# Reordering the vector engine's work around the layer-norm scale, and the first weights, in a routed adapter kernel

## What is computed

```python
h = gelu(x @ W_down[role] + b_down[role])        # 1024 -> 512, exact gelu
u = h @ W_up[role] + b_up[role]                  # 512 -> 1024
y = x + u
mean, var = mean(y), mean((y - mean) ** 2)       # over the 1024 columns
x = (y - mean) * rsqrt(var + 1e-5) * gamma[role] + beta[role]
```

## Time and profile before

| what | value |
|---|---|
| time, median of 3 runs | 2749.48 us (2748.82 to 2749.53) |
| time of the profiled execution | 2748.52 us |
| its span | 2746.7 us |
| mean granted clock of TensorE | 0.992 |
| PE busy | 2686.8 us, 98% |
| DVE busy | 2209.5 us, 80% |
| ACT busy | 1669.8 us, 61% |
| POOL busy | 1388.9 us, 51% |
| down matmuls on PE (L517), each of three kinds | 812 to 813 us |
| HBM traffic | 207 GB/s over the span |

### The profile page before, as it was taken

One profiled execution on the slowest core, in us unless ns is written; L12 is line 12 of the kernel. 1 busy time (PEld: TensorE's weight loads), 2 busy tenths in 40 slices (PEclk: granted clock), 3 DMA queues, 4 the chain that ended last, 5 costly groups with the idle time before them and its releaser, 6 DMA issues.

```text
span 2746.7 us, 54496 instructions
## 1 busy us (share of the span) xinstructions
PE 2686.8 (98%) x11714; PEld 2207.3 (80%) x11714; DVE 2209.5 (80%) x3357; ACT 1669.8 (61%) x2905; POOL 1388.9 (51%) x1050
## 2 busy tenths in 40 slices
PE   8999999999999999999989999999989999999997
PEld 6888888887788888888768888888778888888885
DVE  6777777778777777777898888888888888888886
ACT  4666656666666665665656656665656566665664
POOL 1455555455555555555545454454444455545545
PEclk9999999999999999999999999999999999999998
DMA  6656656566665666656756566666756665666654
GB/s 224 211 193 215 212 199 213 203 230 227 216 215 201 206 209 205 214 199 225 243 185 223 193 215 213 196 212 206 250 184 216 200 223 195 217 204 203 216 190 149
DMA packets 360582, 573.29 MB, mean 209 GB/s; under 512 B 40144, under 2 KB 239952, under 8 KB 359248
## 3 DMA queue, kind: packets, MB, share of 16 engines
q1 hardware_dynamic: 358704, 554.14, 60.3%
q10 hardware_dynamic: 1440, 15.47, 1.5%
HBM read 364.97 MB, written 204.47 MB: 207 GB/s over the span
## 4 chain that ended last, share of the span: by engine, by line
PE 88%; DVE 6%; issue 4%; ACT 1%; DVEq 1%; POOL 0%; DMA 0%; ACTq 0%; POOLq 0%; SPq 0%
PE pD L517 47%; PE bX L529 23%; PE bZ L529 18%; DVE wul L863 1%; DVE xt L961 1%; DVE hl L943 1%; DVE xT L914 1%; DVE wdl L844 0%; DVE xt L953 0%; DVE xl L921 0%; DVE hT L928 0%; DVE xt L984 0%; ACT wdh L601 0%; ACT pC L705 0%; DMA xt<-in_itok 0%
## 5 line engine op out<-in xcount | busy, mean ns | idle before, releaser
L517 PE MATMUL pD<-wdh,xh 128*128 128x512 f32 x2080 | 813.2, 391 | 18.9 <-DVEq L905 18.9
L517 PE MATMUL pD<-wdl,xh 128*128 128x512 f32 x2080 | 812.1, 390 | 0.0
L517 PE MATMUL pD<-wdh,xl 128*128 128x512 f32 x2080 | 812.0, 390 | 0.0
L462 POOL TENSOR_TENSOR xt<-xt,cgb 128x1024 f32<-128x1024 f32 x258 | 629.1, 2439 | 348.7 <-ACT xt L713 348.7
L470 POOL TENSOR_TENSOR cs<-hT 128x256 f32<-128x256 f32 x130 | 154.0, 1185 | 907.4 <-DVE hT L928 907.4
L705 ACT ACTIVATE pC<-xt,nmean 128x512 f32<-128x512 f32 x520 | 358.9, 690 | 260.6 <-DVE nmean L969 251.6
L713 ACT ACTIVATE xt<-xt,rstd 128x1024 f32<-128x1024 f32 x258 | 296.5, 1149 | 319.3 <-POOL rstd L448 315.6
L517 PEld LDWEIGHTS pD<-wdh,xh 128*128 128x128 f32 x2080 | 392.2, 189 | 103.7 <-DVEq L905 16.5
L517 PEld LDWEIGHTS pD<-wdh,xl 128*128 128x128 f32 x2080 | 392.2, 189 | 82.0
L517 PEld LDWEIGHTS pD<-wdl,xh 128*128 128x128 f32 x2080 | 392.3, 189 | 81.5
L529 PE MATMUL bX<-wuh,hh 128*128 128x512 f32 x1040 | 408.4, 393 | 16.3 <-DVE xt L953 8.2
(11 more groups left out here) (106 smaller groups left out, 3819.7 us busy)
## 6 DMA issues: line engine op xcount, KB each, us to landing
xq<-in_xB SPq DMA_DIRECT2D x130, 512.0 KB, 3.5
htok<-hg SPq DMA_DIRECT2D x260, 256.0 KB, 2.8
hq<-htok SPq DMA_DIRECT2D x1040, 64.0 KB, 2.1
xt<-in_x SPq DMA_DIRECT2D x130, 512.0 KB, 4.1
mid<-xt SPq DMA_DIRECT2D x130, 512.0 KB, 3.6
xq<-mid SPq DMA_DIRECT2D x520, 128.0 KB, 3.1
xt<-mid SPq DMA_DIRECT2D x130, 512.0 KB, 4.1
out<-xt SPq DMA_DIRECT2D x128, 512.0 KB, 3.0
```

Source lines behind the costliest of these rows:

```text
L462: eng.tensor_tensor(xt[:, k, :], xt[:, k, :], cgb[:, 1, :], ALU.add).then_inc(s_o, 1)
L517: last = eng.matmul(pD[e][:, :], a[:, e, 128 * k:128 * k + 128], w[:, k, :], start=False, stop=(k == 7 and n == 2), skip_group_check=True)
```

## The change

It has four parts.

1. **Start.** PE clears the banks more than once, ahead of the counting matmuls and behind them. The first group of the first down product waits for one low quarter of the weights (`s_wdl`), the second for two (`s_wd[0]`). ACT waits for the bias only in front of the first `seed_d`. DVE sets up its registers before it waits for the items.
2. **Up weights.** The low parts for products 5 and 6 move out of `take_wu_2` into a new `take_wu_3` with a semaphore of their own, so that product 4 waits for its own low part only. `take_wu_3` and `factors` stand behind last4. The difference b11 = t2 - b11 moves from `take_wu_0` to `take_wu_1`.
3. **Down weights.** On DVE `take_wd_1` stands ahead of the transposes of h. On ACT `take_wd_0` stands ahead of the two seeds, and `take_wd_1` moves into the half step before, ahead of the last two squares.
4. **Every step.** On DVE last4 stands ahead of both scales; scale 0 follows it, and scale 1 stands behind last5. In the last steps last4 and last5 come first, then scale 0, low_h 1, scale 1, last6.

The diff, without the registers' setup on DVE and the moved lines of ACT's bias wait:

```diff
@@ PE, start
-            for bank in bX + [bZ]:
-                last = eng.matmul(bank[:, :], zero[:, 0:128], zero[:, 0:K], start=True, stop=True)
-            last.then_inc(s_bits, 1)
+            for bank in bX + [bZ] + bX:
+                eng.matmul(bank[:, :], zero[:, 0:128], zero[:, 0:K], start=True, stop=True)
             eng.wait_ge(s_oh, 2)
...
+            for bank in [bZ] + bX + [bZ]:
+                last = eng.matmul(bank[:, :], zero[:, 0:128], zero[:, 0:K], start=True, stop=True)
+            last.then_inc(s_bits, 1)
@@ down
-                    if e == 0 and q % 2 == 0:
+                    if i.first() and e == 0 and q == 0:
+                        eng.wait_ge(s_wdl, 1)
+                    elif i.first() and e == 0 and q == 1:
+                        eng.wait_ge(s_wd[0], 1)
+                    elif e == 0 and q % 2 == 0:
                         count(eng, s_wd[q // 2], i, 1, 1)
@@ product
-                    count(eng, s_wu[min(n // 2, 2)], u, 1, 1)
+                    count(eng, s_wu[(0, 0, 1, 1, 2, 3, 3)[n]], u, 1, 1)
@@ ACT, end(i)
                 normal(u + -1, 1)
+                if not (i + 1).first():
+                    kinds.when_new(i + 1, take_wd_0)
                 seed_x(w)
                 seed_z(w)
-                if not (i + 1).first():
-                    kinds.when_new(i + 1, take_wd_0)
                 square(u, 0, 0)
                 square(u, 0, 1)
                 high_h(w, 3)
+                kinds.when_new(i + 1, take_wd_1)
                 square(u, 1, 0)
@@ DVE, take_wu_2 and the new take_wu_3
             def take_wu_2(p):
+                low_wu(eng.snap(pg[2].reg) * 7, 4, b11)
+                eng.wait_ge(s_wul, eng.snap(pg[2].reg) * 7 + 5)
+                eng.sem_inc(s_seen, 1)
+
+            def take_wu_3(p):
                 c = pg[2].next()
-                low_wu(c * 7, 4, b11)
                 low_wu(c * 7, 5, b21)
                 low_wu(c * 7, 6, t4)
@@ DVE, begin(i)
                 onto(u, 1, X, 0, 0)
+                kinds.when_new(i, take_wd_1)
+                ready(i, s_wd[1])
                 transpose_h(w, 0)
                 transpose_h(w, 1)
-                kinds.when_new(i, take_wd_1)
-                ready(i, s_wd[1])
                 low_x(i, 1)
@@
-                kinds.when_near(w, factors)
                 if not u.last():
                     variance(u + -1)
-                if only_up(i):
-                    low_h(w, 1)
-                scale(u + -1, 0)
-                scale(u + -1, 1)
                 last_onto(u, 4, bZ, 0, 1, 3)
+                kinds.when_new(u, take_wu_3)
+                ready(u, s_wu[3])
+                kinds.when_near(w, factors)
+                if not only_up(i):
+                    scale(u + -1, 0)
                 transpose_x(i + 1, 0)
                 last_onto(u, 5, X, 1, 1, 2)
+                if only_up(i):
+                    scale(u + -1, 0)
+                    low_h(w, 1)
+                scale(u + -1, 1)
                 kinds.when_new(w, take_wu_0)
```

More of the change, by code:

```diff
@@ L152, in routed_adapters @@
         s_wul = sem("s_wul")
-        s_wu = [sem(f"s_wu{k}") for k in range(3)]
+        s_wu = [sem(f"s_wu{k}") for k in range(4)]
         s_sub = sem("s_sub")
@@ L573, in _ @@
             pd = [Phases(eng, f"ac_pd{g}") for g in range(2)]
-            pb = Phases(eng, "ac_pb")
+            pb = Phases(eng, "ac_pb", 1)
             pg = [Phases(eng, f"ac_pu{g}") for g in range(2)]
@@ L587, in load_bias @@
                 row = adapter(p)
+                pb.next()
                 count(eng, s_sd, p + -1, 2, 2)
                 eng.dma_start(cbd[:, :], bd[row, :].broadcast_to([128, K])).then_inc(s_bd, 16)
-            def bias_landed(p):
-                eng.wait_ge(s_bd, pb.next() * 16 + 16)
-                eng.sem_inc(s_seen, 1)
             def high_wd(p, c, q):
@@ L662, in seed_d @@
                         eng.wait_ge(s_bits, 1)
+                    if e == 0:
+                        eng.wait_ge(s_bd, eng.snap(pb.reg) * 16)
                     count(eng, s_hg, p + -1, 2, e + 1)
@@ L716, in _ @@
             high_x(Pair(0), 0)
-            bias_landed(Pair(0))
             seed_d(Pair(0), 0)
@@ L775, in link @@
                 eng.wait_ge(s_p, chain[0])
+            kinds = Kinds(eng, "ve_kind")
+            pd = [Phases(eng, f"ve_pd{g}") for g in range(2)]
+            pt = Phases(eng, "ve_pt")
+            pg = [Phases(eng, f"ve_pu{g}") for g in range(3)]
             n0, n1, par0, par1, own, pos, edge = (ct[:, n:n + 1] for n in range(7))
@@ L835, in _ @@
             eng.wait_ge(s_kind, 1)
[L836 to L839, removed]
             def low_wd(c, q):
@@ L880, in take_wu_0 @@
                 low_wu(c * 7, 1, b12)
-                eng.wait_ge(s_wul, c * 7 + 1)
-                eng.tensor_tensor(b11, t2, b11, ALU.subtract).then_inc(s_sub, 1)
                 eng.wait_ge(s_wul, c * 7 + 2)
@@ L891, in take_wu_1 @@
                 low_wu(c * 7, 3, b22)
+                eng.wait_ge(s_wul, c * 7 + 1)
+                eng.tensor_tensor(b11, t2, b11, ALU.subtract).then_inc(s_sub, 1)
                 eng.wait_ge(s_wul, c * 7 + 4)
```

1 line of the change is left out of this document (removed).

## The result

| | before | changed |
|---|---|---|
| median of 4 runs each | 2749.40 us | 2793.41 us (2792.19 to 2795.89) |
| ratio to before, 95% interval | | 1.0163 (1.0151 to 1.0176) |
| span of the profiled execution | 2746.7 us | 2790.4 us |
| mean granted clock | 0.992 | 0.993 |

The change makes the kernel slower by 44 us, 1.6%. The forecast was 2778; the measured time lies in its wide range of 2738 to 2795, near the upper end, and 2 us outside the narrower 2763 to 2791.

The account below looks back on a forecast made before the run. PE's stream of matmuls, busy 98% of the span, was taken as the bound. Start, first weights, turns and switches, with plain and last steps at 0, summed to +28.3 us: 2777.8 us, range 2738 to 2795, narrower 2763 to 2791.

Parts of the forecast that it names:

- switches: The three weight switches: added DVE work is partly exposed for lack of slack, +4.6, +3.6 and +4.0 us.
- turns of layer 0: DVE's late start at the loop body's end, no longer fully covered by slack: .5 us, eight times, +4.0 us.
- turns of layer 1: The same late start in layer 1, with less slack: four of 2.5 us and four of 2.1, +18.4 us.
- Start and first weights: PE's third down group starts earlier, -2.1 us; product 5 of the first pair no longer waits as long, -4.2 us.
- Plain steps: Ordinary steps: scale 1 held by the shift, mean at S+18.2, .15 us of slack left in layer 1, cost 0.
- Last steps: The program's end: product 5 waits less, but the last shifts and power end no earlier; 0, between -3 and +1 us.
- No stop of 3.2: Sign expected in the last steps: PE no longer stops up to 3.2 us in front of product 5.
- Rival 1: Faster: the shift does not hold scale 1, turns keep their cover, 2739.5 us; chance .20.
- Rival 2: Slower still: plain steps of layer 1 don't fit in PE's period, +14 us, 2792 us; chance .14.
- Rival 3: The clock: layer 1 turns that stop PE bring lower-clock stretches, 1.7 us each, eight times, 2792 us; chance .06.
- Rival 4: Half as dear: DVE catches up during PE's stops, turns +10 and switches +6 us, 2763 us; chance .13.

Follow-up runs that it names:

- e1: The changed kernel with both scales back ahead of last4 in all steps but the last ones: 2748.04 us, ratio 0.9997.
- e2: The kernel before with only the order of the scales changed (last4 ahead of scale 0, scale 1 behind last5), last steps as before: 2792.51 us, ratio 1.0157.
- e7: The changed kernel with scale 1 right behind scale 0, both behind last4 and ahead of last5: 2762.03 us, ratio 1.0048.
- e11: The changed kernel with each shift of POOL in two instructions of 512 columns: 2758.49 us, ratio 1.0032.
- e5: The changed kernel with DVE's take_wd_0 and the increment PE's next down product waits for moved ahead of the loop's turn: 2795.71 us, ratio 1.0170.
- e4: The changed kernel with POOL's shift cut from 1024 columns to one, leaving beta out of the others: 2724.44 us, ratio 0.9908.
- e12: The kernel before with POOL's shifts in two instructions of 512 columns and nothing else changed: 2740.89 us, ratio 0.9971.
- e3: The kernel before with the start's part alone, bank clears and the first group waiting for one low quarter: 2746.55 us, ratio 0.9989.

## Why the prediction was right, and where it was off

The mechanism was right: scale 1 is held by shift 0, the mean comes late, and the turns and switches pay for it. The sum was short by 15.4 us (28.3 for 43.7 in the profiled executions), half of it in one term: turns of layer 0 7.7, switches 4.9, turns of layer 1 2.3, the rest .5. That the total stayed in the stated range owes something to its width.

- **Start and first weights** came as worked out: -2.3 for -2.1, -3.9 for -4.2. Product 5 started at 63.60; the 65.6 of the forecast was counted without the 2.1 won at the start, and is 63.5 with it. last4 had not been late.
- **Plain steps** cost nothing, as forecast, with the mean at S+18.3 for S+18.2 and scale 1 at 3.14 for 3.05. Here the working held at every instruction to within some .2 us. e1 and e2 show that it is the order, e7 and e11 that it is the hold.
- **What a turn costs** follows from one time: when DVE's hl behind the stall starts, counted from product 0 of the step before the turn. In layer 0 nothing is lost up to S+21.5, and from there on all of it: 1.3 to 1.6 us for S+22.8 to 23.1 in the changed kernel, .9 to 1.2 for S+22.4 to 22.7 in e5, .6 to .8 for S+22.1 to 22.2 in e11, nothing for S+21.0 in e7 and S+19.9 in the kernel before. In layer 1 it is the same from S+20.0 on (S+20.3 in the kernel before and in e2), so that four turns of the kernel before already cost .25 each, the one at 1552 among them, at which the forecast had PE lose nothing. Means over the eight turns of layer 1, the cost against the kernel before:

| kernel | mean at S+ | stall, us | hl behind it at S+ | us a turn |
|---|---|---|---|---|
| e4 | 16.49 | 3.5 to 4.0 | 20.4 | 0.2 |
| e1 | 15.89 | 4.1 to 4.7 | 20.6 | 0.4 |
| e11 | 17.21 | 4.1 | 21.5 | 1.4 |
| e7 | 17.07 | 4.2 to 4.8 | 21.8 | 1.6 |
| e2 | 18.21 | 4.0 to 4.6 | 22.6 | 2.1 |
| changed | 18.33 | 3.9 to 4.3 | 22.7 | 2.6 |
| e5 | 18.33 | 3.9 to 5.2 | 23.1 | 3.0 |

- **Turns of layer 1** cost 20.7 for 18.4.
- **Turns of layer 0** are the term that was mis-sized: 11.7 for 4.0. In "3.62 less 1.66 of slack less 1.3 for which hl1 no longer waits" the slack was right: in the kernel before the hl starts at S+19.9, 1.6 ahead of S+21.5. The step that failed is the first number. The stall was taken to stay at 3.62, and it took 4.25 to 4.53 in eight of the nine turns. e11 shows what the term comes to without that: its mean in layer 0 is as late as the changed kernel's (S+18.3), its stall is 3.60 to 3.67, and a turn costs .6 to .8, near the .5 forecast. So the longer stall makes some 6 of the 7.7 us missed.

```profile
317.39 1.29 DVE L951 TENSOR_TENSOR hl<-cs,hh 128x512 fp32r<-128x512 f32 x2 [3.64 <-issue]
```

Why the stall grows is open. It doesn't go with the lateness of the mean: e11, as late, has 3.6, and e12, whose mean comes at S+15.9, has 4.25 in layer 0 (there without a loss, since its hl starts at S+20.4). Nor does it go with the order: e2, with nearly the program of before, has 4.2 to 4.5, and e7, with nearly the changed one, 3.6. In e1 and e4 it differs from turn to turn, by 1.0 and 1.9 us. What PE meets first at such a turn is the increment for its down group at S+21.76, then, in products 1 to 3, onto in pieces of .1 to .2 us that no wait row lists: .95 in the row, 1.5 in the starts of the steps. That the increment comes first decides nothing, as e5 shows.
- **Switches** cost 17.1 for 12.2, most of the miss at the boundary (6.3 for 3.6). The 2.6, .6 and 1.4 put in for the weights' parts had no working behind them, the 18.3 us of DVE that a switch was said to add were 22.8 to 24.2 in the rows of the kernel before, and new holds weren't counted. The timeline at the boundary, first a row of the kernel before at the same place:

```profile
1393.42 4.56 DVE L863 TENSOR_TENSOR wul<-rwu,wuh 128x1024 fp32r<-128x1024 f32 x2
...
1408.79 2.85 POOL L462 TENSOR_TENSOR xt<-xt,cgb 128x1024 f32<-128x1024 f32 x1 [5.38 <-ACT xt L719]
...
1409.29 6.77 DVE L866 TENSOR_TENSOR wul<-rwu,wuh 128x1024 fp32r<-128x1024 f32 x2
...
1417.09 0.50 PE L536 MATMUL bX<-wuh,hh 128*128 128x512 f32 x1 [2.57 <-ACT bX L678]
```

Two low up parts, 2.37 together where no shift runs (at 676 us of the kernel before) and 4.56 at this place there, take 6.77: with scale 1 ahead of them, both meet a shift, and seed_x, which waits for the increment behind them, lets PE stop 2.57. In e11 this wait on `bX`'s seed shrinks from 5.0 to 0.6 us.

The clock has a part in it too. Over the three switches PE is busy 6.6 us longer with the same matmuls, which is more than a third of the 17.1 (columns as in the earlier trace rows, summed over the stretches of the table, the kernel before first):

```profile
sum 514.41, PE 484.88 PEld 391.79 DVE 434.04 ACT 318.44 POOL 257.91; mean PE 161.63 PEld 130.60 DVE 144.68 ACT 106.15 POOL 85.97
...
sum 531.54, PE 491.49 PEld 394.04 DVE 467.60 ACT 321.38 POOL 222.88; mean PE 163.83 PEld 131.35 DVE 155.87 ACT 107.12 POOL 74.29
```

The granted clock is at its lower level for 27 us there, and for 17 in the kernel before.
- **Last steps**: +0.3 for 0. The rows:

```profile
2748.87 0.58 ACT L678 ACTIVATE bX<-cbu 128x512 f32<-128x512 f32 x1
...
2749.55 0.76 PE L536 MATMUL bX<-wuh,hh 128*128 128x512 f32 x1 [2.92 <-issue]
...
2776.48 4.65 POOL L462 TENSOR_TENSOR xt<-xt,cgb 128x1024 f32<-128x1024 f32 x2 [6.04 <-ACT xt L719]
```

seed_x ends at 2749.45, product 0 starts at 2749.55: the stop of 3.2 in front of product 5 has become one of 2.92 in front of product 0. "No stop of 3.2" was true of its place only. PE's last step still starts 3.3 us earlier, counted from the step 124 of each kernel, but the last shifts, counted so, start 1.1 us later than in the earlier trace rows. The end hangs on them, as forecast, and nothing is won.
- **Rival 1** (no hold) is refuted by the 3.14 of scale 1 and by e7 and e11. The rule that it goes by, in "Advanced Engine Details and Errata" of the Trainium skill, section on VectorE performance modes, names only two-port Vector modes as those that block; by it the scale would have kept its 1.28, and the trace disagrees. The other, "SBUF — State Buffer", section "SBUF: two separate sides", says that an operation with two SBUF inputs is held for the whole of GpSimd's instruction; e11 agrees, where the hold shrank with the instruction. Its 2739.5 came true in no kernel without a held scale: e1 is at 2748 and e7 at 2762. **Rival 2** (plain steps of layer 1 don't fit) and **rival 3** (the clock) both gave 2792, near what was measured, by other ways: no plain step lost time, and the clock doesn't fall at the turns. The groups behind the turn's stop at 319 start 1.50 and 1.36 us apart, at the upper clock, and in layer 1 a turn has two short stops (.4 to .8 and 1.24 us). The lower clock shows at the switches and in the last steps alone, as behind the stop of 2.57 at 1417.09, whose group takes 2.06. **Rival 4** (half as dear) is out: turns and switches came dearer than forecast, not cheaper.

## What to carry to other kernels

Before an instruction is moved, list what runs on GpSimd where it will land, not only what runs where it stood: here 1.3 us of VectorE became 3.1 in each step. Where slack covers a stall, ask how long the stall can become, and don't take one length for fixed: here its growth made 6 of the 15 us that the forecast missed. And where two engines hold each other by instruction, cutting the uncritical engine's instruction into pieces is a cheap cure: two lines gave 8.7 us to a kernel in which nothing else was touched.

## What the hardware showed that was not expected

- A long GpSimd instruction of 2.40 us in two or four pieces costs less than one: DVE's holds shrink to a piece, and GpSimd takes its turn behind DVE's instruction (a half of 1.3 us took 2.28 behind a scale).
- DVE's stall at a loop's turn isn't fixed: in layer 0 it is 3.6 us in the kernel before, in e7 and in e11, and 4.2 to 4.5 in the changed one, in e2 and in e12, and in layer 1 it goes from 3.5 to 5.2 over all kernels.
- Bank clears ahead of and behind the counting matmuls kept the granted clock at its upper level of 2.4 GHz for the first down product (.23 us a matmul from the second on), where the kernel before ran at the lower one behind an idle of 5.57. e3, with this part alone, kept it up too.
